# A fused block with gated cross-attention, self-attention and four experts: the exact scores in two row halves of TensorE, and the order of the work written out anew

## The reference, cut to what matters

```python
x = x + tanh(g0) * xattn(ln(x), ctx)          # 16 heads of 8, keys from ctx, softmax, @ Wo
h = ln(x)                                     # "the state"
q, k, v = heads(rms(h) @ wq.T), heads(rms(h) @ wk.T), heads(rms(h) @ wv.T)
s = rms(q) @ rms(k).T / sqrt(8), causal       # 16 heads of 8, per sequence
h = h + softmax(s) @ v @ wo.T                 # but not in the first 32 columns
xf = rms(h)
moe = sum of 4 experts of xf, two kept per row by their gate
x = x + tanh(g1) * (h + moe)                  # the first 32 columns without moe
```

## Time and profile before

| what | value |
|---|---|
| median of 3 runs | 1074.19 us (1071.29 to 1077.75) |
| the profiled execution: its time, and the span from its first to its last instruction | 1072.52 us, 1070.7 us |
| TensorE's mean granted clock in it | 0.987 of full speed |
| busy: TensorE, VectorE, ScalarE, GpSimd | 1004.9, 789.2, 736.1, 337.8 us |
| instructions in the trace | 26205 |

### The profile page before, as it was taken

The page is one execution under the profiler, slowest core; times in us unless marked ns, Lnnn a source line. Parts: engine busy times, 40 slices in busy tenths (PEclk is TensorE's granted clock), DMA queues, the critical chain, the costliest instruction groups (busy, mean ns, idle before and its releaser), DMA issues.

```text
span 1070.7 us, 26205 instructions
## 1 busy us (share of the span) xinstructions
PE 1004.9 (94%) x8649; PEld 626.3 (58%) x8649; DVE 789.2 (74%) x2172; ACT 736.1 (69%) x1334; POOL 337.8 (32%) x463
## 2 busy tenths in 40 slices
PE   6678799999999999999999999999999999999898
PEld 5445456566665656666565666656566665655565
DVE  8667777877787787778778777877877777774723
ACT  6466677676777767677776767777676777767453
POOL 5615134051513405151240515124051512404130
PEclk9989899999999999999999999999999999999999
DMA  7433432233343233434323343432234343221200
GB/s 233 134 106 130 136 112 93 90 102 127 115 142 111 90 92 103 127 115 140 109 92 92 106 127 115 136 109 93 90 111 127 115 135 109 82 67 62 69 1 20
DMA packets 77317, 114.28 MB, mean 107 GB/s; under 512 B 7776, under 2 KB 40160, under 8 KB 77152
## 3 DMA queue, kind: packets, MB, share of 16 engines
q1 hardware_dynamic: 76800, 111.53, 33.0%
q10 hardware_dynamic: 480, 2.26, 0.6%
HBM read 58.97 MB, written 53.74 MB: 105 GB/s over the span
## 4 chain that ended last, share of the span: by engine, by line
PE 64%; DVE 15%; ACT 11%; issue 7%; DMA 1%; SPq 1%; POOL 0%; DVEq 0%; ACTq 0%
PE ps_pv L1362 9%; PE ps_w L1388 9%; PE ps_s2a L1341 7%; PE ps_s2b L1341 5%; PE ps_s2a L1400 5%; PE ps_s2b L1407 4%; PE ps_t L1224 4%; ACT probs L951 4%; PE ps_w L1407 3%; DVE mpadB L1091 3%; PE ps_w L1273 3%; DVE mpadA L1091 3%; PE ps_t L1375 2%; PE ps_w L1224 2%; PE ps_w L1305 2%
## 5 line engine op out<-in xcount | busy, mean ns | idle before, releaser
L951 ACT ACTIVATE probs<-ps_s2a 120x512 f32<-120x512 f32 (+1 forms) x256 | 153.4, 599 | 73.1 <-PE ps_s2a L1341 64.7
L1091 DVE TENSOR_REDUCE mpadB<-ps_w 128x4 f32<-128x512 f32 x240 | 148.8, 684 | 24.9 <-PE ps_w L1305 24.9
L1091 DVE TENSOR_REDUCE mpadA<-ps_w 128x4 f32<-128x480 f32 x224 | 131.5, 651 | 38.0 <-PE ps_w L1305 38.0
L951 ACT ACTIVATE probs<-ps_s2b 120x512 f32<-120x512 f32 (+1 forms) x256 | 153.6, 600 | 0.0
L818 POOL TENSOR_SCALAR_AFFINE_SELECT probs<-probs 128x1024 f32<-128x1024 f32 x128 | 139.8, 1092 | 0.0
L1388 PE MATMUL ps_w<-W,hid 128*128 128x96 f32 x976 | 122.5, 279 | 1.0 <-DVE split_k L985 0.9
L1388 PEld LDWEIGHTS ps_w<-W,hid 128*128 128x128 f32 x976 | 114.9, 193 | 10.4 <-issue 4.9
L786 POOL TENSOR_TENSOR rB<-vrB,neg_half 128x4 f32<-128x4 f32 x16 | 16.1, 1007 | 207.2 <-DVE veB L978 207.2
L1341 PE MATMUL ps_s2a<-qdA,kstA 128*120 128x512 f32 x128 | 68.7, 537 | 7.0 <-ACT probs L951 3.1
L1400 PE MATMUL ps_s2a<-hid,W 128*128 128x512 f32 x152 | 74.4, 604 | 0.0
L1120 DVE SCALAR_TENSOR_TENSOR ym<-ps_w,gates,ym 128x96 f32<-128x96 f32 x184 | 45.7, 311 | 38.5 <-PE ps_w L1388 38.5
(11 more groups left out here) (279 smaller groups left out, 2166.7 us busy)
## 6 DMA issues: line engine op xcount, KB each, us to landing
scratch_Aq<-split_q SPq DMA_DIRECT2D x48, 256.0 KB, 2.4
qdA<-scratch_Aq SPq DMA_DIRECT2D x64, 192.0 KB
scratch_Bq<-split_q SPq DMA_DIRECT2D x48, 256.0 KB, 2.4
scratch_Bk<-split_k SPq DMA_DIRECT2D x48, 256.0 KB, 2.9
qdB<-scratch_Bq SPq DMA_DIRECT2D x64, 192.0 KB
kstB<-scratch_Bk SPq DMA_DIRECT2D x64, 192.0 KB
scratch_Ak<-split_k SPq DMA_DIRECT2D x48, 240.0 KB, 2.3
kstA<-scratch_Ak SPq DMA_DIRECT2D x64, 180.0 KB
```

Of the source, the lines that this page charges most:

```text
L951: nc.scalar.activation(probs[0:k, slot_of(part, *index), :], bank[0:k, :], ACT.Exp, scale=SCALE if part == "A" else 1.0).then_inc(done, 1)
L1091: nc.vector.tensor_reduce(pair[:, :, c, b % 2] if halves else mneg[p][:, :, c, b], bank[:, 0:HT * k].rearrange("p (h k) -> p h k", h=HT), ...
```

## The change

The stacks are laid out in two halves of the array's rows. Rows 0 to 47 hold heads 0 and 1 of a tile's four, rows 64 to 111 heads 2 and 3, and rows 48 and 112 the maxima; `qd` has two blocks of columns instead of four. A pair is now four instructions of 256 columns, each with 49 rows at row 0 or row 64 of the array: heads 0 and 1 of tile c to `s2a`, heads 2 and 3 of c to `s2b`, then the same two of tile c+1. So each bank holds two heads of both tiles, the pair waits for both banks before its first instruction, and both are full at its end. `pv` reads `probs` accordingly.

The order is written anew. In the loop no two pairs follow each other directly any more; `pv` of a sequence is cut in two (`early_values`, `late_values`), and so are `down` 0 and 3 (`head`, `rest`). The estimates stand at other places, the sum `out` and, in the loop, the norm of x (`N norm`) come later. In step 1 the first exact scores now stand ahead of the state's transposes (`hT`), and in step 2 the norm of x stands ahead of the pair (0,2) of part A. Some fills of `qd` with zeros before the first step are gone or half as long.

```diff
 def cross_attention():
-    return (exact("A", 0, 0) + one("B", "v") + down(2) + exact("A", 0, 2) + one("N", "xT")
-            + exact("A", 1, 0) + estimate("B", 0) + exact("A", 1, 2)
-            + one("D", "norm", 0, None) + one("B", "init", 0, None) + one("B", "copy", 0, None) + values("A", 0)
-            + exact("A", 2, 0) + estimate("B", 1) + exact("A", 2, 2)
-            + values("A", 1) + down(3) + one("M", "store", 0, None) + one("D", "xfT")
-            + exact("A", 3, 0) + one("A", "oT", 0, "t") + estimate("B", 2) + exact("A", 3, 2)
-            + values("A", 2) + one("D", "logits") + one("A", "nT", 0, "t"))
+    return (exact("A", 0, 0) + one("B", "v") + down(2) + exact("A", 0, 2) + one("N", "xT") + one("D", "squares", 0, None)
+            + estimate("B", 0) + one("D", "out", 0, None)
+            + exact("A", 1, 0) + values("A", 0) + one("D", "norm", 0, None) + one("B", "init", 0, None) + one("B", "copy", 0, None)
+            + exact("A", 1, 2) + head(3) + early_values("A", 1)
+            + exact("A", 2, 0) + rest(3) + one("M", "store", 0, None) + late_values("A", 1)
+            + exact("A", 2, 2) + one("D", "xfT") + estimate("B", 1)
+            + exact("A", 3, 0) + one("A", "oT", 0, "t") + early_values("A", 2) + estimate("B", 2)
+            + exact("A", 3, 2) + one("D", "logits") + late_values("A", 2) + one("A", "nT", 0, "t"))
...
 def third_group():
-    return (one("B", "hT") + exact("A", 0, 0) + exact("A", 0, 2)
-            + one("B", "qk", 0) + one("B", "qk", 1) + one("B", "qk", 2) + one("B", "qk", 3) + one("A", "mL", 0, "t")
-            + exact("A", 1, 0) + exact("A", 1, 2) + one("B", "squares", 0, None) + one("B", "copy", 0, None) + values("A", 0)
+    return (exact("A", 0, 0) + exact("A", 0, 2) + one("A", "mL", 0, "t") + exact("A", 1, 0) + values("A", 0) + one("B", "hT")
+            + exact("A", 1, 2) + one("B", "qk", 0) + one("B", "qk", 1) + one("B", "qk", 2) + one("B", "qk", 3)
+            + one("B", "squares", 0, None) + one("B", "copy", 0, None)
...
-        qd = {p: sb("qd" + p, [P, HT, NT, TOK], F32R) for p in "AB"}
+        qd = {p: sb("qd" + p, [P, HT // 2, NT, TOK], F32R) for p in "AB"}
...
-                        for bk, v in st.drains([], key):
-                            pe.wait_ge(drained[bk], v)
-                        o = bank[0:k, :].rearrange("p (h q) -> p h q", h=HT)
-                        mm(o, kst[p][:, c, b * k:(b + 1) * k], qd[p][:, :, c, b * P:(b + 1) * P],
-                           start=True, stop=True).then_inc(done, 1)
+                        if c % 2:
+                            continue
+                        tiles = [(part, "s2", (b, c + half)) for half in range(2)]
+                        for tile in tiles:
+                            for bk, v in st.drains([], tile):
+                                pe.wait_ge(drained[bk], v)
+                        for cc in range(2):
+                            for half in range(2):
+                                rows = slice(half * HALF_ROWS, half * HALF_ROWS + M_ROW + 1)
+                                o = psum[st.bank[tiles[half]]][0:k, cc * 2 * P:(cc + 1) * 2 * P].rearrange("p (h q) -> p h q", h=2)
+                                ins = mm(o, kst[p][rows, c + cc, b * k:(b + 1) * k], qd[p][rows, :, c + cc, b * P:(b + 1) * P],
+                                         start=True, stop=True)
+                                if cc:
+                                    ins.then_inc(filled[st.bank[tiles[half]]], 1)
```

More of the change, by code:

```diff
@@ L89, in estimate, with values, early_values, late_values @@
     return [(part, "s1", (b, c), rings[c]) for c in range(NT)]
-def values(part, b):
-    return [(part, "pv", (b, c), "pv" if b % 2 and c == NT - 1 else None) for c in range(NT)]
+def values(part, b, first=0, last=NT):
+    return [(part, "pv", (b, c), "pv" if b % 2 and c == NT - 1 else None) for c in range(first, last)]
+def early_values(part, b):
+    return values(part, b, 0, PACK)
+def late_values(part, b):
+    return values(part, b, PACK, NT)
 def one(part, work, index=0, ring="w"):
@@ L134, in cross_attention @@
[L134 to L142 removed]
+HEADED = (0, 3)
@@ new lines, in head, with rest, down @@
+def head(e):
+    return one("M", "head", e, None)
+def rest(e, ring="w"):
+    return fill("M", "down", e, ring)
+def down(e, ring="w"):
+    return (head(e) if e in HEADED else []) + rest(e, ring)
+def self_attention():
+    return (one("N", "load", 0, None) + one("N", "ctx", 0, None) + exact("D", 0, 0) + one("B", "hT") + down(1)
+            + exact("D", 0, 2) + one("B", "qk", 0) + one("B", "qk", 1) + early_values("D", 0)
+            + exact("D", 1, 0) + one("B", "qk", 2) + one("B", "qk", 3) + late_values("D", 0)
+            + exact("D", 1, 2) + one("B", "squares", 0, None) + estimate("A", 0) + early_values("D", 1)
+            + exact("D", 2, 0) + head(0) + late_values("D", 1)
+            + exact("D", 2, 2) + one("B", "sums", 0, None) + rest(0) + one("D", "oT", 0, "t")
+            + exact("D", 3, 0) + early_values("D", 2) + estimate("A", 1) + one("D", "nT", 0, "t") + late_values("D", 2)
+            + exact("D", 3, 2) + one("A", "base", 0, None) + one("B", "root", 0, None))
@@ L1039, in step @@
                             dve.wait_ge(xf_ready, g)
+                            dve.wait_ge(y_ready, g)
                         for b in range(G):
@@ L1347, in step @@
                         last = (part, "pv", (b | 1, NT - 1))
-                        sources = [(part, "s2", index)] if part == "A" else []
+                        sources = [(part, "s2", (b, c // 2 * 2 + half)) for half in range(2)] if part == "A" else []
                         if part == "D":
```

87 lines of the change are left out of this document (39 added, 48 removed).

## The result

The changed kernel takes **1163.48 us** (median of 4 runs, 1162.34 to 1165.06), against 1073.89 us for the kernel before in the same comparison. The ratio is 1.083 (95% interval 1.081 to 1.085). The forecast was 1109 us, in a range of 1045 to 1150. Its sign was right, its size was not: the kernel became 90 us longer and not 37, more than twice as much, and the time lies above the range.

A forecast was written before the change was run, and what follows sets the result against it. TensorE, busy 732 of the loop's 750 us, was taken as the bound. Cross-attention +2.1 and the rest +0.3 made 2.4 us a pass; 14 passes 34, other steps 3: 37 on 1072.5 gives 1109 us, range 1045 to 1150.

The forecast's parts named there:

- Pairs and halves: Exact-score pairs on TensorE: 0.22 us in row halves instead of 0.46, so 16 pairs save 3.84 us a pass.
- rival 2: Weight loads of the two halves follow each other: +2.5 us a pass, about 1145 us; 0.15 together with the clock rival.
- Crossings: TensorE changing array tiles in the loop: 0.1 us into a strip, 0.2 into the whole array; 4.8 us more a pass.
- Rival 1: Crossings of the halves cost nothing: +0.4 us a pass, about 1080 us; chance 0.15.
- Waits, cross-attention: From B's `v` to the group behind `nT`: three estimates wait 1.1, 1.2, 1.0 us; stage 19.7 us, +2.1.
- Rival 3: Faster: no three cross-attention waits and free crossings, about 1018 us, or 1050 with half-price crossings; 0.2 with half-way forms.
- The rest of the pass: Loop outside cross-attention: 9 pairs save 2.2 us, crossings add 2.8, waits go from 2.9 to 2.6; +0.3 a pass.
- Rival 4: Clock falls as TensorE is less busy in cross-attention; 0.95 adds about 2.5 us a pass; 0.15 with the weight-load rival.
- The steps outside the loop: Steps 2 and 15 cost 2.4 us each like loop passes; steps 0, 1, 16 and 17 add 3 us together.
- step 0: Pipeline filling, pairs close together: a pair waits for both banks, then ScalarE waits for the next pair; 2 us more.
- step 1: Scores move ahead of a wait for the state's norm: 2 us saved, bounds 0 and -4.
- Step 2: Step outside the loop, taken to have the loop's order and so to cost the same 2.4 us more.

The follow-up runs named there:

- Run 1: The change's new order without the halves, with scores, layout and fills of the kernel before: 1127.38 us, ratio 1.049 to the kernel before.
- run 7: The kernel before, except that the first tile of each pair waits until both of the pair's banks are empty: 1099.93 us, ratio 1.026.
- Run 6: The changed kernel with four idle matmuls ahead of each of the first three estimates of part B: 1152.96 us, ratio 1.073 to the kernel before.
- run 9: The kernel before with stack rows at 0 to 47 and 64 to 111, gap included, and maxima in row 48 alone: 1077.39 us, ratio 1.004.
- run 10: The kernel before with the wait of a pair's first tile for both banks, and stack rows in two blocks with a gap: 1107.27 us, ratio 1.030.
- run 14: New order with the scores of the kernel before, but steps 1 and 2 in their old order: 1120.41 us, ratio 1.045 to the kernel before.
- run 2: The halves with their layout and loads, in the order of the kernel before: 1118.39 us, ratio 1.039 to the kernel before.
- run 8: The kernel before with stack rows in two blocks of 48 rows without a gap: 1075.58 us, ratio 1.003.

## Why the prediction was right in sign and wrong in size

**Pairs and halves.** Right in mechanism: rival 2 (weight loads one after the other) falls with the rows of cross-attention. By its sign alone, a pair of 0.45 us, it would nearly stand, for a pair takes 0.42; but the loads of the two halves start within 0.01 us of each other. The starts of the rounds are 0.21 us apart where I had 0.11, since the first weights are loaded from the start that is shown on and not ahead of it (546.25 and 546.26 us); I had them in the sum.

**Crossings.** Right where TensorE doesn't wait. The reason given for the dearer one is in before's trace: the weight loads of a whole-array group start 0.09 and 0.11 us ahead of its first matmul behind another such group (419.14 and 419.23, 431.31 and 431.42 us), but with it behind strips (both at 422.38, both at 441.34). Those of B's `v` behind a pair of the change start at 543.40, its first matmul at 543.41. Between whole-array groups a pair takes 0.42 us, `down` ahead of it 1.86 where it was 1.71, and B's `v` behind a pair 0.99 where it was 0.89: 0.67 us in all, so the two crossings cost 0.45 where I had 0.4, and a pair there costs 0.21 more than the 0.46 of before. Rival 1 (they are free) falls. But over a pass TensorE's busy time falls by 0.8 us (60.42 against 61.19) where I had its work grow by 1.0. Run 1 has nine more crossings for no more busy time, and run 7, with the work of before, has 1.0 less: I take from this that a crossing or a weight load that falls into a wait costs nothing, but no run shows that by itself. So the 4.8 us were too much for a kernel that waits this often.

**Waits, cross-attention.** The three waits were right: 1.1, 1.2 and 1.0 us predicted, 1.17, 1.34 and 1.07 measured, and 0.33 ahead of the logits that I had missed. Rival 3 falls with them: it needed xnT to end within 1.1 us of the pair's start, and it took 2.1. From B's `v` to the group behind `nT` it is 20.5 us, predicted 19.7; in the pass at the full clock it is 20.4. TensorE's busy time in this stretch, before and after:

```profile
430.53:448.14 17.61, 17.18 (x197) 12.09 (x196) 14.23 (x35) 13.49 (x27) 2.42 (x3) 1.00 0.62 194
273.03:293.40 20.37, 16.29 (x213) 11.84 (x211) 16.13 (x41) 13.40 (x26) 3.50 (x4) 1.00 0.63 167
```

For the change my sum was near: 16.2 us of work against 16.3, and 3.5 of waits against 4.1 (0.3 ahead of the logits, 0.3 in the three). What failed is *"so waits about 1.7"*: I took the waits before as what unit prices left over. TensorE idled for 0.4 us there, and for only 1.34 in the whole pass, by the earlier trace rows, which I had in hand. So the old work was 1.3 us more than I had, and it fell by 0.9 where I had it grow by 0.3. That 16.2 came near is luck: the two errors cancel. I should have subtracted busy from length first and fitted the prices to that.

**The rest of the pass.** +0.3 predicted; 3.4 for the pass less 2.8 for this stretch is +0.6. The same wrong remainder (2.9 us of waits) stood in it. I had its waits fall by 0.3 us; TensorE's idle time outside the stretch rose from 0.9 to 1.4. Over the whole pass I had waits grow by 1.5 us, and they grew by 4.1; I had work grow by 1.0, and it fell by 0.8.

**The clock.** Rival 4 had the mechanism and its size for a clock of 0.95 (2.5 us); it came with my forecast and not in place of it: +1.4 us a pass at 0.97, some 16 us in eleven passes. My sum had nothing for it: I weighed it as an alternative and gave it, with rival 2, only 0.15. Run 6 shows that these 1.4 us hang on TensorE's waits.

**The steps outside the loop.** This is the step that failed worst. Up to the fourth reciprocal my terms are +2 for step 0, -2 for step 1 and 2.4 each for steps 2 and 3, some 5 us; 30 were lost. *"Transfers change in shape only (two rows for the maxima instead of one): 0"* doesn't hold: with the gap the transfers take longer in every trace, and the first pair starts some 2 to 3 us later (28.42 in the change against 26.49; run 9). The *2* for step 0 and its wait for both banks: by the first reciprocal run 7 has 4.4 us, and 6.5 with the loads (run 10); by the fourth it is 9.7 and 15.0. Step 1, *"I take -2"*: with the new order its first reciprocal came 1.9 to 3.3 us later than with the old one, since the scores ahead of hT stand waiting for their stacks (2.5 us in run 1). Step 2, *"the loop's order"* and so +2.4: run 14 shows 5.9 us between the second and the third reciprocal, since there the estimates of part A wait for maxima. I costed what is repeated with care and what happens once by the handful.

**In sum.** Of the 90 us, the first steps lost 30, where I had 5. Eleven passes lost 53, where I had 26: 37 at the full clock (3.4 each) and some 16 by the clock. The last steps lost 7, where I had 5. Three terms, idle time, clock and first steps, each came in above its line, with only the work and its crossings on the other side.

**What stays open:** why some passes get a stretch at the lower clock and others not. The old cross-attention order with halves idles for 4.1 us in 64.0 and has none; with xT in bank t it is 3.75 in 64.2 and has many. Filling the waits removes them, but neither the sum of the idle time nor its longest piece orders these kernels. The losses of the first steps are read as differences of starts between single executions, so their shares are known to a microsecond or two.

## What to carry to other kernels

Before pricing a change of order, subtract an engine's busy time from the stretch's length: that is all the waiting there is to win, and any remainder of unit prices above it means that a price is wrong. A layout that makes two consumers share one start (here two banks for one pair) has its price in waits: by itself that start made a pass 1.7 us longer (run 7), and the waits ate what the halves saved (2.7 us of work a pass saved, 3.8 us of idle time added, run 2). Steps that run once deserve their own walk, step by step and with their loads: here they made a third of the loss.

## What the runs showed of the hardware

Two f32 matmuls of 49 rows in the two row halves start within 0.01 us of each other, with their weight loads, and the next round follows 0.21 us on (546.26 and 546.47 us). The clock fell to half (0.50 granted, from 563.6 to 567.0 us) in a pass whose longest single wait of TensorE was 1.34 us, and with four idle matmuls ahead of the first three estimates of part B it stayed at 1.00 through a pass (524.2 to 590.1 us, run 6). And loads of 24 rows each kept the transfer engines longer when they went to rows 0 to 47 and 64 to 111 than to rows 0 to 95 (37.9% against 33.0% of the span for the same 111.53 MB, runs 9 and 8), and the first pair, which waits for them, started 2.4 us later than with two blocks without a gap.
